# Soft rows of the router turned by VectorE and moved by transfers, with an earlier norm for some routers and a reordered start, in a macaron block (MoE, gated linear attention, MoE)

## What is computed

```python
x = x + 0.5 * ffn(layernorm(x))
x = x + attn(layernorm(x))
x = x + 0.5 * ffn(layernorm(x))
```

```python
flat = w_e[:, inv_map]                       # [tokens, 8, 8]
scalar = flat.sum(-1)
soft = softmax(where(flat == 0, -1e9, flat)) # over the 8 of a group
xg = x[:, None] + einsum('ngi,ghi->ngh', soft, mask_up_w)
g, u = xg @ gate_proj_w[g].T, xg @ up_proj_w[g].T   # 352 columns a group
y = einsum('ng,ngh->nh', scalar, einsum('ngi,ghi->ngh', silu(g) * u, down_proj_w))
```

## Time and profile before

| what | value |
|---|---|
| median of 3 runs | 1843.44 us (1840.55 to 1846.49) |
| the profiled execution | 1840.89 us, of which the span is 1839.1 us |
| TensorE matmuls | 8432, busy 1817.5 us (99%) |
| VectorE, ScalarE, GpSimd busy | 873.4, 520.7, 185.2 us |
| mean granted TensorE clock | 0.998 of full |
| transfers | 378.36 MB, mean 206 GB/s |

### The profile page before, as it was taken

How to read it: one execution, slowest core, us unless ns; L and a number is a source line. 1 busy time by engine, 2 the same in 40 slices (tenths; PEclk the granted TensorE clock), 3 DMA queues, 4 the chain that set the end, 5 groups by cost and what they waited for, 6 DMA issues and landing times.

```text
span 1839.1 us, 22152 instructions
## 1 busy us (share of the span) xinstructions
PE 1817.5 (99%) x8432; PEld 1513.8 (82%) x8432; DVE 873.4 (47%) x1621; ACT 520.7 (28%) x780; POOL 185.2 (10%) x334
## 2 busy tenths in 40 slices
PE   7999999999999999999999999999999999999999
PEld 5887888888888888888888888888888888888887
DVE  7566454565355663324444665354664324422222
ACT  3324322542124432112212533124432111311111
POOL 1131120110010100001010110010010001000000
PEclk9999999999999999999999999999999999999999
DMA  5987765555475555377656565475455467556664
GB/s 195 380 289 268 264 210 202 173 195 173 141 228 173 171 198 178 134 257 235 228 178 218 183 218 172 163 231 166 155 195 199 137 219 260 206 174 228 232 235 167
DMA packets 97384, 378.36 MB, mean 206 GB/s; under 512 B 14496, under 2 KB 14880, under 8 KB 76544
## 3 DMA queue, kind: packets, MB, share of 16 engines
q1 hardware_dynamic: 54288, 268.66, 41.8%
q10 hardware_dynamic: 27792, 47.20, 9.3%
q0 software_dynamic: 15200, 61.09, 9.0%
HBM read 323.55 MB, written 41.81 MB: 199 GB/s over the span
## 4 chain that ended last, share of the span: by engine, by line
PE 93%; DVE 3%; DMA 2%; SPq 1%; issue 1%; ACT 1%; POOL 0%; ACTq 0%; DVEq 0%
PE bank L1123 27%; PE bank L1125 27%; PE bank L1124 27%; PE bank L1329 4%; DMA x_lo<-tb 1%; SPq L314 1%; PE bank L1269 1%; PE bank L1261 1%; PE bank L1255 1%; PE bank L1268 1%; PE bank L1152 1%; PE bank L1153 0%; PE bank L1314 0%; PE bank L1315 0%; PE bank L1160 0%
## 5 line engine op out<-in xcount | busy, mean ns | idle before, releaser
L1123 PE MATMUL bank<-x_hi,wt 128*128 128x512 f32 x1328 | 522.4, 393 | 0.0
L1125 PE MATMUL bank<-x_lo,wt 128*128 128x512 f32 x1328 | 518.0, 390 | 0.0
L1124 PE MATMUL bank<-x_hi,wt 128*128 128x512 f32 x1328 | 517.7, 390 | 0.0
L722 DVE TENSOR_TENSOR act_t<-bank,sig 128x512 f32<-128x512 f32 x176 | 121.5, 690 | 521.9 <-PE bank L1329 462.8
L1125 PEld LDWEIGHTS bank<-x_lo,wt 128*128 128x128 f32 x1328 | 249.6, 188 | 52.8
L1124 PEld LDWEIGHTS bank<-x_hi,wt 128*128 128x128 f32 x1328 | 249.9, 188 | 50.8
L1123 PEld LDWEIGHTS bank<-x_hi,wt 128*128 128x128 f32 x1328 | 249.9, 188 | 50.4
L1123 PE MATMUL bank<-dt,a_hi 128*128 128x512 f32 x704 | 278.1, 395 | 0.3 <-DVE a_lo L722 0.3
L1125 PE MATMUL bank<-dt,a_hi 128*128 128x512 f32 x704 | 274.7, 390 | 0.0
L1124 PE MATMUL bank<-dt,a_lo 128*128 128x512 f32 x704 | 274.5, 390 | 0.0
L646 ACT ACTIVATE sig<-bank 128x512 f32<-128x512 f32 x176 | 105.2, 598 | 542.5 <-PE bank L1329 542.4
(11 more groups left out here) (182 smaller groups left out, 1703.9 us busy)
## 6 DMA issues: line engine op xcount, KB each, us to landing
wt<-scr_w SPq DMA_DIRECT2D x140, 1152.0 KB, 5.2
dt<-scr_d SPq DMA_DIRECT2D x140, 512.0 KB, 5.1
s_bc<-scr_s ACTq DMA_DIRECT2D x128, 256.0 KB, 4.8
state<-wat POOLq DMA_DIRECT2D x28, 512.0 KB, 6.4
scr_w<-wt POOLq DMA_DIRECT2D x12, 1024.0 KB, 7.7
b_all<-wgu SPq DMA_DIRECT2D x22, 512.0 KB, 8.3
scr_d<-dt POOLq DMA_DIRECT2D x22, 512.0 KB, 4.3
scr_w<-tw POOLq DMA_DIRECT2D x10, 1024.0 KB, 7.6
```

Source lines behind the costliest of these rows:

```text
L722: return nc.vector.tensor_tensor(dst, a, b, op)
L1123: mm(dst, wh, xh, start=start, stop=False)
L1124: mm(dst, wl, xh, start=False, stop=False)
L1125: return mm(dst, wh, xl, start=False, stop=stop)
```

## The change

Four things change together.

- **Soft rows.** In phases 1 to 7 the route is no longer turned by TensorE. VectorE turns its high and low parts in squares of 32 x 32 (128 x 256 elements each), in place of making the repeated columns with two copies. Sixteen transfers of 32 KB a phase bring the squares to `softT`: eight by SyncE at chunk 17, eight by GpSimd (behind the RMS step of head 1 in a phase with attention, after the squares in one without; at chunk 15 in phase 0). TensorE's two batches of four transposes and ScalarE's two copies go. Logits and scalars are copied with their tokens reordered, so that a logit tile is now a tile of tokens. The sums for the scalars are made first in slot 44.
- **Norm up.** For the routers of phases 1, 4 and 7, built in the phases 0, 3 and 6: statistics from slot 27 to 21, norm from 30 to 24, split from 36 to 33, SyncE's moves of the squares from chunk 12 to 10. In phase 0 GpSimd's `rstd_of` goes from chunk 9 to 7 and its moves from 10 to 8. The load of block 3's tokens goes from chunk 6 of phase 3 to chunk 2.
- **Tokens first.** SyncE waits for the third token tile before it asks for weights, and asks for both raw gate and up chunks first, then the mask, then the down weights.
- **Fold sooner.** Four of the eight masked matmuls of chunk 0 now come after the folds, and VectorE's second raw split comes after the fold matrix.

```diff
+        def stat_slot(p):
+            return 27 if p - 1 in ATT else 21
         def norm_slot(p):
-            return 31 if p - 1 in ATT else 30
+            return 31 if p - 1 in ATT else 24
+        def split_slot(p):
+            return 36 if p - 1 in ATT else 33
...
+            def move_soft(p, first):
+                sp.wait_ge(route_ok, p + 1)
+                for b in (first, first + 1):
+                    for j, src in enumerate((soft_hi, soft_lo, soft_hi, soft_hi)):
+                        sp.dma_start(softT[cols(j, Q), p % 2, :, cols(b)].bitcast(F32),
+                                     src[cols(b, Q), :, :, :].rearrange("p h i t -> p h (i t)")).then_inc(soft_in[first // 2], 16)
...
             for i in range(NT):
                 sp.dma_start(xr(0)[:, i, :], x_t[0][:, i, :]).then_inc(ld_x0[i], 16)
+            sp.wait_ge(ld_x0[NT - 2], 16)
             raw_gate_up(0)
+            raw_gate_up(1)
+            sp.dma_start(mask.rearrange("p a b -> p (a b)"), c_mask).then_inc(ld_mask, 16)
             raw_down(0)
-            sp.dma_start(mask.rearrange("p a b -> p (a b)"), c_mask).then_inc(ld_mask, 16)
-            raw_gate_up(1)
             raw_down(1)
...
-                    if c == 12 and p + 1 < PHASES:
+                    if c == (12 if p in ATT else 10) and p + 1 < PHASES:
                         move_squares(LN_R[p + 1], (p + 1) % 2)
-                    if p == 3 and c == 6:
+                    if c == 17 and p + 1 < PHASES:
+                        move_soft(p + 1, 0)
+                    if p == 3 and c == 2:
                         sp.wait_ge(o_ok, 2 * H)
...
                     if h:
                         rms(t, h - 1)
+                    if h == 2:
+                        move_soft(q + 1, 2)
...
-                elif k in (49, 50):
+                elif k in (49, 50) and p == 0:
...
+                    if p:
+                        step(nc.vector.tensor_copy(r_c.bitcast(F32R), r_a))
+                        step(tt(r_b, r_a, r_c, ALU.subtract))
+                        wait(dve, u_ok, (p - 1) * CH)
+                        for dst, src in ((soft_hi, r_c), (soft_lo, r_b)):
+                            ins = nc.vector.transpose(dst.rearrange("p h i t -> p i h t"), src.rearrange("p i (h e) -> p i h e", h=2))
+                        ins.then_inc(route_ok, 1)
+                        return
...
-                elif k in (49, 50):
+                elif k in (49, 50) and p == 0:
...
+                elif p and c == chunk(p * CH):
+                    for i in range(2):
+                        pe.wait_ge(soft_in[i], 16 * 2 * NQ * p)
...
-            masked(0)
+            masked(0, 0, KC // 2)
             pe.wait_ge(fold_ok, 1)
             router(0, 39)
+            masked(0, KC // 2, KC)
```

More of the change, by code:

```diff
@@ L152, in build @@
         route = tb_flat[:, 5 * NT * E:5 * NT * E + NT * 2 * P].rearrange("p (t c) -> p t c", t=NT)
-        lgT = tb_flat[:, 5 * NT * E + NT * 2 * P:5 * NT * E + NT * 2 * P + NB]
+        lgT = tb_flat[:, 5 * NT * E + NT * 2 * P:5 * NT * E + NT * 2 * P + NB].rearrange(
+            "p (i b t) -> p i b t", i=NT, b=NQ)
+        soft_hi, soft_lo = (route[:, 2 * i:2 * i + 2, 0:P].rearrange("p h (i t) -> p h i t", i=NT) for i in range(2))
         e_pos, e_neg, e_rest = tb[:, 0:2, :], tb[:, 2:4, :], tb[:, 4:6, :]
@@ L205, in build @@
         sq_in = [sem(f"sq_in{i}") for i in range(2)]
+        soft_in = [sem(f"soft_in{i}") for i in range(2)]
         logit_ok, logit_cp, folded, rmax_ok, exp_ok, gmax_ok, gexp_ok, route_ok, routeT_ok, route_cp = (
@@ L368, in rstd_of, with move_soft @@
                 pool.wait_ge(rstd_ok, (r + 1) * NT)
+            def move_soft(p, first):
+                pool.wait_ge(route_ok, p + 1)
+                for b in (first, first + 1):
+                    for j, src in enumerate((soft_hi, soft_lo, soft_hi, soft_hi)):
+                        pool.dma_start(softT[cols(j, Q), p % 2, :, cols(b)].bitcast(F32),
+                                     src[cols(b, Q), :, :, :].rearrange("p h i t -> p h (i t)")).then_inc(soft_in[first // 2], 16)
             def move_squares(r, s):
@@ L519, in router @@
                 r = LN_R[p]
-                if k in (36, 37) and p:
-                    hi(r, k - 36, p % 2)
+                if k in (split_slot(p), split_slot(p) + 1) and p:
+                    hi(r, k - split_slot(p), p % 2)
                 elif k == 38:
@@ L535, in router @@
                     wait(act, st_s, 16 * p)
-                    copy(scal_row[:], W1[0:G, :]).then_inc(scal_cp, 1)
+                    copy(in_order(scal_row[:]), by_quarter(W1[0:G, :].rearrange("p (i b t) -> p i b t", i=NT, b=NQ))).then_inc(scal_cp, 1)
                     act.wait_ge(scal_cp, p + 1)
                     act.dma_start(scr_s[p % 2], scal_row[:]).then_inc(st_s, 16)
-                elif k in (49, 50):
+                elif k in (49, 50) and p == 0:
                     i = k - 49
[L541 to L544, removed]
+                    act.wait_ge(routeT_ok, i + 1)
+                    copy(in_order(softT[:, 0, i, :]), by_quarter(YB[i + 2][:].rearrange("p (i b t) -> p i b t", i=NT, b=NQ))).then_inc(route_cp, 1)
             def exps(t, pair):
@@ L816, in router @@
                         wait(dve, u_ok, (p - 1) * CH)
+                        for m in range(2):
+                            wait(dve, soft_in[m], 16 * 2 * NQ * (p - 1))
+                        if p == 1:
+                            dve.wait_ge(routeT_ok, 2)
                         if p - 1 in ATT:
@@ L1159, in router @@
                     for i in range(NT):
[L1160 removed]
+                        ins = mm(W1[:, cols(i)], lgT[:, i, :, :].rearrange("p b t -> p (b t)"), fold_m[:], start=True, stop=True)
                     ins.then_inc(folded, 1)
@@ L1166, in router @@
                     ins.then_inc(scalT_ok, 1)
-                elif k in (49, 50):
+                elif k in (49, 50) and p == 0:
                     i = k - 49
[L1169 to L1175, removed]
+                    pe.wait_ge(route_ok, 1)
                     for j in range(NT):
-                        ins = nc.tensor.transpose(b[:, cols(j)], route[:, j, cols(i)], ident[:])
+                        ins = nc.tensor.transpose(YB[i + 2][:, cols(j)], route[:, j, cols(i)], ident[:])
                     ins.then_inc(routeT_ok, 1)
@@ L1307, in weights, with masked @@
                 return hi, lo
-            def masked(c):
+            def masked(c, k0=0, k1=KC):
                 pe.wait_ge(gu_lo_ok, c + 1)
@@ L1312, in masked @@
                 hi, lo = weights(0, c)
-                for k in range(KC):
+                for k in range(k0, k1):
                     mm(W0[:, 0:2 * P], mup[:, c % 2, k, :], hi[:, k, :], start=(k == 0), stop=False)
                     ins = mm(W0[:, 0:2 * P], mup[:, c % 2, k, :], lo[:, k, :], start=False, stop=(k == KC - 1))
-                ins.then_inc(m_mm, 1)
+                if k1 == KC:
+                    ins.then_inc(m_mm, 1)
             def main(b, c0, p, c):
@@ L1325, in soft @@
                     pe.wait_ge(m_ok, c + 1)
-                if c in (chunk(p * CH), chunk(p * CH + 1)):
-                    pe.wait_ge(route_cp, 2 * p + c % 2 + 1)
+                if p == 0 and c < 2:
+                    pe.wait_ge(route_cp, c + 1)
+                elif p and c == chunk(p * CH):
+                    for i in range(2):
+                        pe.wait_ge(soft_in[i], 16 * 2 * NQ * p)
                 m = wt[:, c % 2, W_M:WW]
```

45 lines of the change are left out of this document (26 added, 19 removed).

## The result

The changed kernel takes 1833.31 us (median of 7, 1831.67 to 1834.94) against 1840.55 us before (median of 7, the three of the table further up among them). The ratio is 0.9948 with a 95% interval of [0.9934, 0.9963]: 0.52% faster, beyond the 0.3% that a measurement tells. The two medians by themselves stand 7.2 us apart, the ratio gives 9.6 us, and its interval (6.8 to 12.1 us) holds both. The profiled execution took 1832.78 us, its span is 1831.0 us, 8.1 us shorter.

What follows compares the result with a forecast made beforehand. TensorE, busy 1817.5 of 1839.1 us, was taken as the bound; 6.2 + 5.4 + 1.2 = 12.8 us off 1840.9 gave 1828.1, and 1829 us allowing for the median. Range: 1825 to 1836.5 us.

Steps and rivals of the forecast that it cites:

- Part 1, the transposes: Phases 1 to 7: two batches of four TensorE transposes fewer a phase, 0.44 us each, 6.2 us (5.5 to 6.5).
- The unknowns beside it: Soft rows: half-size VectorE turning 0.36 to 0.71 us; moves hidden by some 20 us; weight loads delayed 0 to 2.5 us.
- the sum: Whole kernel: 6.2 + 5.4 + 1.2 = 12.8 us off the profiled execution's 1840.9 us; bounds 9.3 to 14.8 us.
- (c): Start gives nothing and phase 0's moves stay late behind a raw load on SyncE: 1833 to 1836 us; chance 0.10.
- On GpSimd ... No delay.: GpSimd, attention phase: eight issues end at 437.6, before the next mask at 439.38, so they delay nothing.
- one of the signs that the prediction had named for being wrong: TensorE: a wait for `wt`, `dt`, `softT` or raw weights, or a clock of 0.5 in a new place.
- Part 2, the norm up: Routers in phases 0 and 3: waits of 2.42 and 1.36 us and 1.6 us of slow clock go, 5.4 us (lower 3.8).
- Part 3, the start: Start: third token tile before weights, folds before four masked matmuls; 1.2 us taken, bounds 0 to 2.9.
- (a): Waits return elsewhere as ScalarE or VectorE falls behind at chunk 10 or 11: 1834.7, or 1837 us by median; chance 0.12.
- (b): SyncE's eight issues make a weight load late; 10 us late costs 27 us, a time of 1855 us; chance 0.06.
- (d): TensorE was the better place: moved rows too late, each phase's first soft matmuls wait; at 3 us, 1849 us; chance 0.02.

Runs made afterwards that it cites:

- the kernel with twelve: The changed kernel with twelve soft moves a phase on SyncE at chunk 17 and four on GpSimd: 1829.17 us, ratio 0.9932.
- the second set: Four kernels on one chip: changed kernel with GpSimd's program shifted 1833.75 us; soft moves on SyncE with TensorE kept busy 1827.95, with squares issued first 1829.34; changed kernel 1831.63.
- the kernel with the squares ahead of the load: All soft moves on SyncE, and in chunk 4 of attention phases SyncE issues the squares' moves before the `wt` load, against the changed kernel: 1829.34 us, ratio 0.9919.

## Why the prediction was right, and which step failed

**Part 1, the transposes: right.** 14 batches at 0.44 us were to give 6.2 us; putting 14 back costs 7.0 us by medians, where each ratio is known to some 3 us either way. Soft rows alone gained 3.1 us by the ratio (0.9 to 5.3), which fits 6.2 less the 3.4 to 4.5 us of waits that they bring in phases 2 and 5. The unknowns beside it held. A turning of half size takes 0.424 us, between the bounds of 0.36 and 0.71; a 32 KB move lands in 3.1 us on SyncE and 2.8 us on GpSimd in the median, no soft matmul after the start waits, and no weights are late. The Trainium skill's fit in DMA: Bandwidth & Descriptors, "Anatomy of one DMA — SWDGE (gpsimd) path", gives an estimate of 2.1 us for 32 KB; the trace has more.

```profile
L921 DVE STREAM_TRANSPOSE tb<-tb 128x256 f32<-128x256 f32 x14 | 5.4, 424 | 0.2
```

```profile
softT<-tb SPq DMA_DIRECT2D x56, 32.0 KB, 3.1
softT<-tb POOLq DMA_DIRECT2D x56, 32.0 KB, 2.8
```

**The time and the range.** The measured 1833.31 us lies in the range of 1825 to 1836.5 us, but 4.3 us above the 1829 us forecast, and the gain (7.2 us by the medians, 8.1 by the profiles, 9.6 by the ratio) falls short of the sum's 12.8. By the time alone rival (c), with its 1833 to 1836 us, fits better than the forecast. What speaks for the forecast is the rows: its three savings are there, and something that it put at nothing takes a part of them back.

**The step that failed is "On GpSimd ... No delay."** I compared the end of eight issues with the next mask of the same phase, and that comparison held: the issues began at 427.16 and took 4.30 us, and the next mask, at 433.51, still waited for ScalarE. What I did not look at is what the added transfers do to GpSimd's later ones, and which of these is read without slack. The squares of phases 2 and 5 are: the added moves shift the count of transfers, and the 129th and 211th, which start 2.25 and 2.52 us late, are now the first squares of these phases. The cost, a term that the sum put at nothing, is 3.4 us of waits in the profile of the changed kernel; in its second profile it is 3.7 us and a stretch of 3.4 us at half clock behind the second wait, in a place where the kernel before has none. That is one of the signs that the prediction had named for being wrong. With the soft moves on SyncE it is gone (1829.33 us), with a quarter of them left on GpSimd too (1829.17 us). Against the changed kernel's 1833.31 and 1831.63 us that is 2 to 4 us, measured in part on different chips, and the intervals of the ratios overlap; the traces show the mechanism more surely than the times its size.

**Part 2, the norm up: right.** Both waits are gone, and so is the slow clock of phase 0: 5.4 us in the profile, 4.8 us by the ratio of the kernel with this part alone. The split of phase 3 was to end 7.4 us ahead of the logits (853.6 against 861.0 on the clock of before); it ended 8.6 us ahead, at 844.80 + 1.22 = 846.0 against 854.60:

```profile
844.80 1.22 DVE L758 TENSOR_TENSOR x_lo<-x_lo,x_hi 128x1024 fp32r<-128x1024 f32 x1
```

**Part 3, the start: its mechanism right, its size open.** The folds start 2.1 us sooner (20.16 to 18.08), the first soft matmuls 1.6 us. The fourth token tile was in time: its statistics no longer wait, against the earlier trace rows.

```profile
7.79 0.69 DVE L803 BATCH_NORM_STATS2 stats<-x_res 128x6 f32<-128x512 f32 x1
```

The sum kept 1.2 us for it, with bounds of 0 to 2.9. Alone it measured 1.0002, but there the wait of phase 0 took the lead of 1.4 us back, and the changed kernel no longer has that wait. In the changed kernel the lead at chunk 12 of phase 0 is 0.2 us in the first profile (145.03 against 145.26) and 1.1 us in the second (144.19), and the difference is the length of the half clock stretch. That length is not the start's doing: norm alone, with the old start, had the long one, and the start alone the short one. The changed kernel itself had the long one in its first profile (0.51 above) and the short one in its second, in the same window:

```profile
35.20:42.10 6.90, 5.90 (x26) 4.93 (x24) 4.94 (x8) 3.16 (x7) 0.00 (x0) 0.75 0.72 151
```

**The rivals.** (a) had the right shape, waits that come back in another place with about its price (its 1834.7 against a profiled 1832.8), but for another reason: not ScalarE or VectorE at chunk 10 or 11, but GpSimd's queue in phases that the norm's move does not touch. (b) did not happen: even sixteen issues added on SyncE instead of eight made no weights late. The only wait for `wt` in any of these traces is 0.19 us, in the kernel with twelve, and it comes 35 us ahead of that phase's soft moves. (c) did not happen in phase 0, whose wait is gone; its other half, a start that gives nothing, is close to the first profile, where 0.2 us were left. The measured time falls on its 1833 to 1836 us by chance, since what took the gain back is another thing. (d) did not happen. The Trainium skill, VectorE: DVE Perf Modes, "Rules for kernel authors", sends a 128x128 turning to TensorE where its result may go to PSUM. This case differs: with TensorE 99% busy, the way round by VectorE and transfers is the cheaper one, by 7.0 us for 14 batches.

So of the sum's 12.8 us the profile has 12.3 on the side of the gains, but that closeness is partly luck: the start has 0.2 us in it where the sum has 1.2, and 0.5 us are the two small waits that nobody forecast. The 4.25 us of waits, 3.4 of them the change's own, were not in the sum. Of the changed kernel's two sessions one gave 1833.3 and one 1831.6 us; the 1829 us forecast is about what it took with the soft moves off GpSimd's queue (1829.33).

**The fastest version measured** is that with the soft moves on SyncE and TensorE kept busy in the start: 1827.95 and 1828.46 us in two sessions, 0.9913 and 0.9928, against 0.9948 and 0.9935 for the changed kernel; in the second set, where both ran, the intervals overlap. What the busy start adds is 1.4 us by medians of one session (against the kernel with the squares ahead of the load as well), less than the times can tell. The traces tell it: at chunk 12 of phase 0 the three profiles with a busy start are 3.0 to 3.1 us ahead of the kernel before, the changed kernel's two 0.2 and 1.1 us, that with all soft moves on SyncE and nothing else 0.55 us.

```profile
142.17 0.62 PE L1381 MATMUL bank<-softT,wt 128*128 128x512 f32 x2
```

## What to carry to other kernels

On an engine that is busy 99% of the span, every instruction taken off counts in full, and a longer way round through other engines and transfers is free as long as its end has slack and what it puts on a queue delays nothing else. Before work is added to a queue, look beyond its next instruction: for each later one on it, find who reads its result and by how little it arrives in time; such an edge stands in no wait list until it is broken. Where a moved operation could go on either of two queues, try both, and look in the trace which queue got in the way.

## What the runs showed of the hardware that was not expected

**A late start of a GpSimd transfer, by its place in the count.** The usual start behind a wait takes at most 0.56 us. The 129th transfer on GpSimd's queue starts later in every profile here, and with nothing to wait for: 1.10 to 1.12 us in the eight profiles with 194 transfers (that of the kernel before is one), 1.9 us in that with 222, 2.25 to 2.27 us in the four profiles with 250. It is a load of `state` in phase 3, a soft move, or the first squares of phase 2, whatever the program has at that place, and a shift of the program by 32 instructions left it there. With more transfers there is a second such start: the 211th of 250 by 2.52 us, the 207th of 222 by 3.28 us. Why these counts, and what sets the length, stays open.

**Waits of 0.1 to 2.3 us before an attention's first matmuls** come at changing places from profile to profile: 0.2 us in all in the kernel before, 4.0 us in that with the start alone, whose attention phases are the same. The one of 2.15 us at 280.21 stands behind squares of which the last landed 8.95 us after its issue, where the earlier trace rows have 7.45, and behind it the clock stood at half for 3.4 us. These waits set how much one profile can tell of a change of 3 us.

**The half clock in the start** came with the same two waits in each kernel that has them, lasted 3.4 or 6.8 us, both in one and the same program, and was absent in all three profiles in which TensorE had work during the waits. Later in the kernel the same length of wait did not always bring it: 2.09 us before the logits of phase 5 had full clock behind it in the changed kernel's first profile, 2.06 us had 3.4 us at half in its second.
